# Local attention on one core: the clip, the token shift and the output product written in another way

## What is computed

```python
h = shift_token(x)            # features 64..127 come from the token before
q, k, v = split(h @ wqkv)     # 8 heads of 64
q = q / clip(norm(q), 1e-12) * qs
k = k / clip(norm(k), 1e-12) * ksc
q, k = rotary_xpos(q, k)
o = local_attention(q, k, v)  # windows of 64, each looks at itself and the one before
x = x + o @ wo
```

## Time and profile before

| | |
|---|---|
| median of 3 runs | 1549.52 us (1544.6 to 1549.98) |
| profiled execution, own time | 1545.77 us |
| its span | 1544.0 us |
| busy share of the span | PE 80%, PEld 52%, DVE 74%, ACT 56%, POOL 54% |
| attention of the first local layer, first to last q projection | 760.7 to 1022.5 us |
| attention of the second local layer, likewise | 1154.5 to 1412.6 us |

### The profile page before, as it was taken

One profiled execution on the slowest core, in us unless ns is written; L12 is line 12 of the kernel. 1 busy time (PEld: TensorE's weight loads), 2 busy tenths in 40 slices (PEclk: granted clock), 3 DMA queues, 4 the chain that ended last, 5 costly groups with the idle time before them and its releaser, 6 DMA issues. The chain is left out here.

```text
span 1544.0 us, 26296 instructions
## 1 busy us (share of the span) xinstructions
PE 1237.7 (80%) x7828; PEld 800.8 (52%) x7828; DVE 1138.3 (74%) x2560; ACT 865.4 (56%) x2259; POOL 829.3 (54%) x760
## 2 busy tenths in 40 slices
PE   6889999854228988479689988885877998898797
PEld 3333333353116877334257666663555766666465
DVE  1299999847118877356589999982658999999464
ACT  5623333243114544237578878783746887888664
POOL 0064344245750555541177767676746776777663
PEclk9999999967559999869889999997998999999999
DMA  3700000031120122130100000000000000000001
GB/s 113 251 1 0 1 0 1 0 104 44 49 90 1 42 63 65 47 120 1 50 1 3 2 1 1 0 1 1 1 22 1 2 2 2 1 1 1 1 1 55
DMA packets 35031, 44.06 MB, mean 29 GB/s; under 512 B 5621, under 2 KB 24978, under 8 KB 34913
## 3 DMA queue, kind: packets, MB, share of 16 engines
q1 hardware_dynamic: 30304, 34.27, 7.0%
q0 software_dynamic: 4608, 8.47, 1.7%
HBM read 22.65 MB, written 21.12 MB: 28 GB/s over the span
## 5 line engine op out<-in xcount | busy, mean ns | idle before, releaser
L1865 ACT ACTIVATE W<-W,nm 128x128 f32<-128x128 f32 x512 | 197.9, 393 | 0.0
L1648 POOL TENSOR_TENSOR W<-W,rden 128x512 f32<-128x512 f32 x128 | 133.0, 1040 | 117.7 <-DVE rden L1966 111.5
L1633 POOL TENSOR_TENSOR R<-R 128x512 f32<-128x512 f32 x128 | 162.6, 1292 | 34.8 <-DVE R L1936 34.8
L1936 DVE TENSOR_TENSOR R<-bank,tab 128x1024 f32<-128x1024 f32 x128 | 151.0, 1214 | 17.0 <-ACT sq L1831 13.1
L1959 DVE CUSTOM_DVE_ANT_0 W<-bank,mask_q,rn 128x128 f32<-128x128 f32 x512 | 146.3, 338 | 7.7 <-issue 4.2
L1194 POOL DMA_INDIRECT expert_rows<-Yt,xin x80 | 83.2, 1040 | 115.4 <-DVE Yt L1167 89.1
L1849 ACT ACTIVATE QK<-bank 128x512 f32<-128x512 f32 x128 | 75.5, 590 | 68.0 <-PE bank L1720 61.1
L616 DVE TENSOR_TENSOR_SCAN S<-beta,U 128x512 f32<-128x512 f32 x64 | 100.0, 1583 | 0.0
L1865 ACT ACTIVATION_READ_ACCUMULATOR W<-W,nm 128x1 f32 x512 | 98.5, 192 | 0.0
L1770 PE MATMUL bank<-PT,VA 128*64 128x128 f32 (+1 forms) x1024 | 86.3, 262 | 13.9 <-issue 10.9
L1745 PE MATMUL bank<-QK 64*64 64x128 f32 x2048 | 85.8, 282 | 11.6 <-DVE nm L1959 11.3
(11 more groups left out here) (310 smaller groups left out, 3583.3 us busy)
## 6 DMA issues: line engine op xcount, KB each, us to landing
expert_slots<-empty SPq DMA_DIRECT2D x8, 650.0 KB, 6.4
xin<-expert_slots SPq DMA_DIRECT2D x8, 650.0 KB
expert_rows<-empty SPq DMA_DIRECT2D x8, 512.0 KB, 6.7
pair_rows<-expert_rows SPq DMA_DIRECT2D x16, 256.0 KB, 4.2
expert_raw<-w1e_dram SPq DMA_DIRECT2D x9, 256.0 KB, 2.8
expert_raw<-w2e_dram SPq DMA_DIRECT2D x9, 256.0 KB, 3.0
tok<-x_dram SPq DMA_DIRECT2D x8, 256.0 KB, 4.5
out_dram<-tok_out SPq DMA_DIRECT2D x8, 256.0 KB, 2.7
```

The source lines that it names most:

```text
L1633: nc.gpsimd.tensor_tensor(halves[:, :, 0, :, z, :], halves[:, :, 0, :, z, :], halves[:, :, 1, :, 1 - z, :], ALU.add).then_inc(summed, 1)
L1648: nc.gpsimd.tensor_tensor(x, x, scale.to_broadcast([P, 4, P]), ALU.mult).then_inc(scaled, 1)
L1865: m = nc.scalar.activation(x, x, ACT.Exp, scale=-1.0, bias=nm[:, p % RING, j:j + 1], accum_out=den[:, p % RING, j:j + 1])
L1936: nc.vector.tensor_tensor(R[:, i, qk, :, :].rearrange("p c (h d) -> p c h d", d=DH), x, y.to_broadcast([P, 2, HEADS, DH]), ALU.mult).then_ ...
```

## The change

Three edits, all in the attention part of `local_layer`. The clip of the sums of squares, a `tensor_scalar` with a constant, becomes a `tensor_reduce` with max over pairs (sum, constant), the constants being set once. The token shift leaves DVE: the high parts are copies on ACT at the end of rounds 0 and 1 of the step before, the low parts are subtractions on POOL in rounds 1 and 3, behind `mix_values` and ahead of `scale_keys`; the counter `shifted` now rises by two per chunk. The output product, one f32 product per block of features, becomes three fp32r products: DVE keeps a high part of each attention output and subtracts for a low one, and POOL splits the weights `wo2` at the start of a layer.

```diff
@@ pool, start of the layer
+                def shift_low(g, par, part):
+                    hi, lo = hs[0][par], hs[1][par]
+                    early_rows, late_rows = shifted_views(k, here(g))
+                    wait_alone(k, pool, hs_hi, 2 * (g + l) + part + 1)
+                    if part == 0:
+                        nc.gpsimd.tensor_tensor(lo[0:DH, :], early_rows, hi[0:DH, :].bitcast(F32), ALU.subtract).then_inc(shifted, 1)
+                        wait_alone(k, pool, shifted, 2 * (g + l) + 1)
+                    else:
+                        nc.gpsimd.tensor_tensor(later(lo[DH:P, :]), late_rows, later(hi[DH:P, :]).bitcast(F32),
+                                                ALU.subtract).then_inc(shifted, 1)
+                        wait_alone(k, pool, shifted, 2 * (g + l + 1))
+
+                shift_low(G0, 0, 0)
+                shift_low(G0, 0, 1)
+                pool.wait_ge(w_in, L * 16 * len(names))
+                nc.gpsimd.tensor_scalar(wo[0][:], w["wo2"][:], 1.0, None, ALU.mult).then_inc(wo_r, 1)
+                pool.wait_ge(wo_r, 2 * L - 1)
+                nc.gpsimd.tensor_tensor(wo[1][:], w["wo2"][:], wo[0][:].bitcast(F32), ALU.subtract).then_inc(wo_r, 1)
@@ pool, step
                                 mix_values(g, par, t // 2)
+                                shift_low(g + 1, 1 - par, t // 2)
                             scale_keys(g, par, t)
@@ pe
-                            pe.wait_ge(shifted, g + 1 + l)
+                            pe.wait_ge(shifted, 2 * (g + 1 + l))
...
-                        m = nc.tensor.matmul(ps[BO[1]][:, 0:SEQ], w["wo2"][:, b, :], OT[par][:, b, s * SEQ:(s + 1) * SEQ],
-                                             start=(b == 0), stop=(b == NB - 1))
+                        for wp, op in PASSES:
+                            m = nc.tensor.matmul(ps[BO[1]][:, 0:SEQ], wo[wp][:, b, :], OT[op][:, s, b, :],
+                                                 start=(b == 0 and wp + op == 0), stop=(b == NB - 1 and wp == 1))
@@ act
+                def shift_high(g, par, part):
...
+                        nc.scalar.activation(hi[0:DH, :], early_rows, ACT.Copy).then_inc(hs_hi, 1)
+                    else:
+                        nc.scalar.activation(later(hi[DH:P, :]), late_rows, ACT.Copy).then_inc(hs_hi, 1)
+
+                shift_high(G0, 0, 0)
+                shift_high(G0, 0, 1)
...
+                        if project and t < 2:
+                            shift_high(g + 1, 1 - par, t)
@@ dve
+                nc.vector.memset(sums[:, :, :, 1:2], CLIP2)
...
-                    nc.vector.tensor_scalar(ss[:, i, :], ss[:, i, :], CLIP2, None, ALU.max).then_inc(clipped, 1)
+                    nc.vector.tensor_reduce(ss[:, i, :], sums[:, i, :, :], AX.X, ALU.max).then_inc(clipped, 1)
...
-                    nc.vector.tensor_copy(OT[par][:, b, s * SEQ:(s + 1) * SEQ], ps[BO[p % 2]][:, 0:SEQ]).then_inc(o_r, 1)
+                    O = ps[BO[p % 2]][:, 0:SEQ]
+                    nc.vector.tensor_copy(OT[0][:, s, b, :], O).then_inc(o_r, 1)
+                    dve.wait_ge(o_r, 2 * (NPAIR * c + p) + 1)
+                    nc.vector.tensor_tensor(OT[1][:, s, b, :], O, OT[0][:, s, b, :].bitcast(F32), ALU.subtract).then_inc(o_r, 1)
...
-                            shift_part(g + 1, 1 - par, t)
                             rotate(g, t)
```

More of the change, by code:

```diff
@@ L1577, in local_layer @@
             R = k.sb(f"R{l}", [P, 2, 2, 2, CH], ctx=ctx)
+            sums = k.sb(f"sums{l}", [P, 2, 2 * HEADS, 2], ctx=ctx)
             ss = k.sb(f"ss{l}", [P, 2, 2 * HEADS], ctx=ctx)
@@ L1583, in local_layer @@
             PT = k.sb(f"PT{l}", [P, 2, CH], ctx=ctx)
-            OT = [k.sb(f"OT{l}_{i}", [P, NB, CH], ctx=ctx) for i in range(2)]
+            OT = [k.sb(f"OT_{part}{l}", [P, SPC, NB, SEQ], F32R, ctx) for part in ("hi", "lo")]
+            wo = [k.sb(f"wo2_{part}{l}", list(k.dram["wo2"].shape)[1:], F32R, ctx) for part in ("hi", "lo")]
             lnb = k.sb(f"lnb{l}", [P, 1], ctx=ctx)
-            (w_in, made, hs_hi, shifted, proj, v_mm, v_sb, squared, rotated, sums_r, clipped, logged, rnorm, summed,
+            (w_in, wo_r, made, hs_hi, shifted, proj, v_mm, v_sb, squared, rotated, sums_r, clipped, logged, rnorm, summed,
              normed, turned, qk_r, s_mm, s_seen, max_r, exp_r, rden_r, scaled, wT_mm, pt_r, v_mixed, av_mm, o_r, x_mm,
              resid, v_seen, s_free) = map(shared, (
-                 "w_in", "made", "hs_hi", "shifted", "proj", "v_mm", "v_sb", "squared", "rotated", "sums_r", "clipped",
+                 "w_in", "wo_r", "made", "hs_hi", "shifted", "proj", "v_mm", "v_sb", "squared", "rotated", "sums_r", "clipped",
                  "logged", "rnorm", "summed", "normed", "turned", "qk_r", "s_mm", "s_seen", "max_r", "exp_r", "rden_r",
@@ L1762, in weighted_values @@
                         pe.wait_ge(v_mixed, 2 * (SPC * c + s + 1))
-                    need(pe, o_r, NPAIR * c + p - 1)
+                    need(pe, o_r, 2 * (NPAIR * c + p - 1))
                     if b == 1:
@@ L1774, in output @@
                 def output(c, par, s):
-                    pe.wait_ge(o_r, NPAIR * c + NB * (s + 1))
-                    pe.wait_ge(w_in, L * 16 * len(names))
+                    pe.wait_ge(o_r, 2 * (NPAIR * c + NB * (s + 1)))
+                    pe.wait_ge(wo_r, 2 * L)
                     for b in range(NB):
-                        m = nc.tensor.matmul(ps[BO[1]][:, 0:SEQ], w["wo2"][:, b, :], OT[par][:, b, s * SEQ:(s + 1) * SEQ],
-                                             start=(b == 0), stop=(b == NB - 1))
+                        for wp, op in PASSES:
+                            m = nc.tensor.matmul(ps[BO[1]][:, 0:SEQ], wo[wp][:, b, :], OT[op][:, s, b, :],
+                                                 start=(b == 0 and wp + op == 0), stop=(b == NB - 1 and wp == 1))
                     m.then_inc(x_mm, 1)
@@ L1825, in _ @@
                 act.wait_ge(made, L)
+                def shift_high(g, par, part):
+                    hi = hs[0][par]
+                    early_rows, late_rows = shifted_views(k, here(g))
+                    if part == 0:
+                        need(act, v_mm, NTILE * (g - 1))
+                        nc.scalar.activation(hi[0:DH, :], early_rows, ACT.Copy).then_inc(hs_hi, 1)
[3 more added lines that the diff above has]
+                shift_high(G0, 0, 1)
                 def squares(g, t, qk):
@@ L1942, in lengths @@
                     need(dve, rnorm, n - 1)
-                    nc.vector.tensor_reduce(ss[:, i, :], sq[:].rearrange("p q (h d) -> p (q h) d", d=DH), AX.X,
-                                            ALU.add).then_inc(sums_r, 1)
+                    nc.vector.tensor_reduce(sums[:, i, :, 0:1].rearrange("p h o -> p (h o)"),
+                                            sq[:].rearrange("p q (h d) -> p (q h) d", d=DH), AX.X, ALU.add).then_inc(sums_r, 1)
                     dve.wait_ge(sums_r, n + 1)
-                    nc.vector.tensor_scalar(ss[:, i, :], ss[:, i, :], CLIP2, None, ALU.max).then_inc(clipped, 1)
+                    nc.vector.tensor_reduce(ss[:, i, :], sums[:, i, :, :], AX.X, ALU.max).then_inc(clipped, 1)
                 def maxima(c, par, p):
```

## The result

The changed kernel takes 1599.3 us (median, 1598.6 to 1602.4) where the kernel before took 1547.1 on the same chip: a ratio of 1.0343 with a 95% interval of 1.0312 to 1.0374, **52 us slower**. The forecast was slower by 22. The profiled execution took 1602.4, its span is 1600.6, 56.6 more than the span before.

What follows compares the result with a forecast made beforehand. It took DVE, busy 96%, to bound the kernel. Steady steps -7.4, clock +14, first two chunk ends +8.2, layer starts +4.6 and drain +2.7 gave +22 us, so 1572 for the median, range 1552 to 1604.

Steps and rivals of the forecast that it cites:

- The wait at the chunk end: At each steady chunk end PE and then DVE wait for POOL's second low part: DVE 3.9 us, +19.5 per layer.
- The clock: Behind PE's gap at a chunk end its clock falls to about half: 1.0 us per end, 14 ends, +14 us.
- The first chunk end of a layer: At a layer's first chunk end DVE's rotation moves from 790.90 to 793.7, +2.8 us.
- Starts, drains and the end: Outside the chunks: +4.6 us for the starts of two layers and +2.7 for the drain, 7.3 forecast.
- a steady round costs what DVE's operations cost: In the steady rounds of both layers DVE, busy 198.08 of 205.55 us (96%), was taken to set the time.
- DVE gains 21.7 us per layer: DVE's work in a layer's steady steps: shift -20.5, clip -20.5, low part of the attention output +19.3 us.
- the late keys: POOL's low part in round 1 delays `scale_keys` and PE's work behind it: 0.5 us per chunk, +3.0 per layer.
- The DVE work saved in that chunk gives back some 2.6: At a layer's second chunk end, DVE work saved in that chunk offsets some 2.6 of about 3.9 us, leaving +1.3.
- ACT's two copies are covered by ACT's idle 19%: ACT's two shift copies per chunk, 1.1 us, were costed at nothing; without that cover they cost 13 us in all.
- The two branch gaps disappear under the same wait: DVE's idle gaps at chunk ends on the loop's branch vanish: -5.9 us in the first layer, -3.1 in the second.
- the other covers fail: Rival: ACT's copies are not hidden (+13) and the clock costs 1.5 us an end (+7): 1592 us, chance 0.14.
- The wait is covered: Rival: POOL's subtraction ends 3.9 us sooner at chunk ends, so PE feeds DVE in time: 1506 us, chance 0.10.

## Why the prediction was right in direction and short in size

**What held.** The wait at the chunk end: PE idle for 3.64 (4.3 forecast), DVE for 3.90 (3.9), 9.47 from rotation to rotation (9.4), and the early low parts, which undo it, give back the whole loss. Within it the subtraction took 1.09 for 1.28 and began 0.27 behind the copies for 0.08; that these two cancel is luck. The clock: 1.0 in the round behind an end, with a granted 0.57 at its start. The Trainium skill (TensorE: Matmul & The Clock Gate, Terms) has the larger price that the prediction names beside it, half of the throttled time; the run with the added products does not bear that out, 1.0 an end it is. The fall also costs time at places where the forecast had none, below. The clip's 0.186 for 0.2: here the Trainium skill's rule (SBUF — State Buffer, Who interferes with whom) and the trace agree, 0.186 for the tensor_reduce against 0.90 (before) and 0.93 (without the clip's edit) in the mean for the tensor_scalar in its place. The trace shows the wait itself. The clip of the earlier trace rows ends at 854.12 + 0.91 = 855.03, just behind the end, at 854.99, of what POOL was doing:

```profile
853.72 1.27 POOL L1633 TENSOR_TENSOR R<-R 128x512 f32<-128x512 f32 x1
```

In the kernel before 58 of the 64 clips end 29 to 36 ns behind an instruction of POOL; the other six begin just ahead of POOL's next one, by up to 5 ns, and take 0.174 to 0.175. The reduction takes 0.185 to 0.189 in all 64 places. The low part's 0.425. The first chunk end of a layer, +3.4 and +2.7 for 2.8. Starts, drains and the end, 8.4 for 7.3.

**The step that failed** is the one that opens the working, "a steady round costs what DVE's operations cost", and with it "DVE gains 21.7 us per layer" as time. That was near the truth for the kernel before, with DVE at 96%; the change itself took DVE out of that place. From the first rotation of a chunk of the changed kernel to the end of the last:

```profile
1295.03:1322.93 27.90, 25.77 (x288) 20.22 (x288) 25.52 (x83) 25.66 (x87) 20.27 (x19) 0.95 0.01 2
```

PE, DVE and ACT are each busy 92% of it, none of them the bound by itself. DVE's idle time within the three rounds grew from 0.24 to 2.2 us a chunk, 1.9 of it ahead of rotations, for the squares. With the low parts earlier, where the clock is granted in full in nearly every one of these rounds, 1.55 of it remain. The experiments show both halves of this: in the kernel before, less work on DVE gives seven tenths of itself (clip); in the change, more of it costs about half (23 us for 47), with the low parts early 2.4 us less of it in a chunk give 0.5, and moving work from DVE to ACT loses 6 to 10 us.

The 34 us between forecast and result lie in these terms:

- *The steady chunks, 26 us.* DVE's work fell by 17.4 + 18.2 instead of 2 x 21.7: 8. The clip, the shift and the low parts fell and grew as forecast, within 1 us each; the maxima of the scores, which no edit touches, take 0.344 for 0.336 each and their readouts 0.083 for 0.077, 2.2 to 2.5 us a layer, and the rest of the 8 was not taken apart. The waits in the rounds are 2.0 a chunk more than before, where 0.5 for the late keys and 0.8 for the clock were allowed: 0.7 x 12 = 8. The last tile's rotations take 2.64 for 2.36: 3. The branch gaps in the first layer: 6, below. Two ends take 10.1 for 9.46, since the clock falls there ahead of the first product: 1. That makes the 26.
- *The second chunk of each layer.* "The DVE work saved in that chunk gives back some 2.6" was wrong: DVE is not the bound there, rounds 0 and 1 together give back 0.1 to 0.3, and round 2 takes 9.89 and 9.97 where it took 7.86. The two chunks of a layer lose 9.7 where 6 were allowed, 7 us in all. The timeline of that place, rows of POOL, PE and DVE:

```profile
812.79 1.26 POOL L1635 TENSOR_TENSOR hs_lo<-H,hs_hi 64x512 fp32r<-64x512 f32 x1
...
814.18 1.04 POOL L1663 TENSOR_TENSOR R<-R,rn 128x512 f32<-128x512 f32 x1
...
815.37 0.63 PE L1742 MATMUL bank<-ident,R 128*128 128x128 f32 x4 [2.42 <-POOL R L1663]
...
821.34 1.23 DVE L1956 TENSOR_TENSOR R<-bank,tab 128x1024 f32<-128x1024 f32 x1 [1.02 <-ACT sq L1866]
```

The keys stand behind the low part, PE waits 2.42 for them and DVE 1.02 at the next rotation. With the low part behind the keys the round takes 7.84. But the low part itself accounts for only a quarter of the 2.0. In the run with the added products PE waits the same 2.42 there in the first layer, the clock does not fall, and the round takes 8.41. That round in the change and in that run:

```profile
811.45:821.34 9.89, 7.30 (x77) 5.76 (x77) 7.75 (x29) 7.36 (x26) 7.90 (x8) 0.83 0.01 2
793.39:801.80 8.41, 5.82 (x77) 4.63 (x77) 7.56 (x29) 7.12 (x26) 7.92 (x8) 1.00 0.01 3
```

So the low part costs 0.5, which is the 0.5 that the prediction takes for it in a steady chunk, and the clock 1.5, for which it had no term at this place. The other runs with the low part there agree: 8.3 to 8.6 at a full clock and 9.9 to 10.0 at 0.83. Why the clock falls behind this wait in some runs and not in others stays open.

**Covers.** "ACT's two copies are covered by ACT's idle 19%" failed: that share was an average. In rounds 0 and 1 the copy stands right ahead of the next tile's squares. ACT and DVE in round 1 of the same chunk as above:

```profile
1310.83 0.63 ACT L1857 ACTIVATE hs_hi<-H 64x510 fp32r x1
1311.48 0.60 ACT L1866 ACTIVATE sq<-bank 128x512 f32<-128x512 f32 x1
1312.20 1.23 DVE L1956 TENSOR_TENSOR R<-bank,tab 128x1024 f32<-128x1024 f32 x1 [0.19 <-ACT sq L1866]
...
1313.13 0.58 ACT L1866 ACTIVATE sq<-bank 128x512 f32<-128x512 f32 x1
1313.83 1.23 DVE L1956 TENSOR_TENSOR R<-bank,tab 128x1024 f32<-128x1024 f32 x1 [0.41 <-ACT sq L1866]
```

The squares start when the copy ends and DVE waits for both of them. What that costs in the change itself is not shown: the earlier copies took back 4 us or nothing. In the kernels without late low parts it is 6 to 10. "The two branch gaps disappear under the same wait" is right in the second layer (9.46 and 10.13 at the branch, as elsewhere) and wrong in the first (12.32 and 12.89): there the pause does not lie under the wait but behind it, in the middle of the projection that everybody waits for:

```profile
907.25 0.49 PE L1721 MATMUL bank<-wqkv_hi,hs_hi 128*128 128x512 f32 x1 [3.64 <-POOL hs_lo L1638]
...
907.58 0.40 PE L1721 MATMUL bank<-wqkv_hi,hs_lo 128*128 128x512 f32 x1
...
910.27 0.80 PE L1721 MATMUL bank<-wqkv_lo,hs_hi 128*128 128x512 f32 x1 [2.29 <-issue]
```

PE has 2.29 us of "issue" between the second product and the third. The pause does not belong to the layer as such: with the shift alone, with PE kept busy and with both low parts late, the ends at the branch take no longer than the others in either layer. What decides it was not found.

**The rivals.** The time, 1599, lies next to "the other covers fail" (1592) and inside the range. That it lies there is in part luck. Its first half, ACT's copies, cost 6 to 10 us for the 13 named in kernels beside the change, and were not priced in the change itself. Its second half, a dearer clock, was found at other places than named: round 2 of the second chunk, 1.5 in each layer, and four ends of 10.1, 0.7 each, some 6 us for the 7 named. "The wait is covered" is what the early low parts make of the change: 0.9905, not the 0.97 that the prediction gave it, again because the rounds do not follow DVE's work.

The best of these kernels is the clip alone, or with the low parts early on POOL and the high parts left on DVE: 0.984 and 0.982 of the time before, not told apart.

## What to carry to other kernels

When an edit takes work off the busiest engine, ask what the share of the next two engines is in the same stretch: here three engines came to stand at 92%, and from there a microsecond of work added to DVE cost about half of itself, and in a near variant one removed gave a fifth. An idle share covers an added operation only where it stands in front of nobody: look at what is queued directly behind it. And before work moves to another engine's queue, ask when its first consumer needs it; the same two subtractions behind the keys of rounds 1 and 2, instead of ahead of those of rounds 1 and 3, were worth over 4% here. A new wait of PE has two prices, its own and that of the clock that may fall behind it: 0.5 and 1.5 us in the second chunks.

## What was not expected of the hardware

The pause at the loop's branch is not on DVE alone: PE had 2.29 us of "issue" between two products of one projection, in the first layer and not in the second, so that a wait ahead of it hides nothing there; three other kernels with a late low part show no such pause at all. And a GpSimd subtraction on 64 lanes and two runs of 255 columns took 1.09 (L1638) where 64 lanes and one run of 512 took 1.26 (L1635) and 85 lanes 1.28; why was not tried.
